# Gated-attention block on eight cores: transposes, evictions and waits of the attention stage reordered, and the loading of W1 moved to another queue

## What is computed

```python
hv = silu(layernorm(x) @ W_h + b_h)                 # 1024 -> 4096
v, gate = hv[..., :HID], hv[..., HID:]
qk = silu(layernorm(x) @ W_qk + b_qk)               # 1024 -> 128, then four heads by gamma, beta
attn = square(relu(einsum('bgid,bgjd->bgij', quad_q, quad_k) / 256 + bias))
quad_out = einsum('bgij,bgje->bgie', attn, v)        # inside a group of 256 tokens
lin_kv   = einsum('bgnd,bgne->bde', lin_k, v) / n    # over the whole sequence
lin_out  = einsum('bgnd,bde->bgne', lin_q, lin_kv)
out = gate * (quad_out + lin_out)
x2 = layernorm(out @ W_o + b_o + 2 x)                # 2048 -> 1024
y  = layernorm(x2 + relu(x2 @ W1 + b1) @ W2 + b2)    # 1024 -> 4096 -> 1024
```

## Time and profile before

| | us |
|---|---|
| median of three runs | 2604.03 |
| lowest and highest of them | 2598.41, 2815.92 |
| the profiled execution, its own time | 2597.35 |
| its span on the slowest core (core 4) | 2595.8 |
| spans of the eight cores | 2580.8 to 2595.8 |

### The profile page before, as it was taken

How to read it: one execution, slowest core, us unless ns; L and a number is a source line. 1 busy time by engine, 2 the same in 40 slices (tenths; PEclk the granted TensorE clock), 3 DMA queues, 4 the chain that set the end, 5 groups by cost and what they waited for, 6 DMA issues and landing times.

```text
span 2595.8 us, 27752 instructions; the slowest of 8 cores (2580.8 to 2595.8 us)
## 1 busy us (share of the span) xinstructions
PE 2083.8 (80%) x9498; PEld 876.5 (34%) x9498; DVE 541.0 (21%) x1127; ACT 731.5 (28%) x1192; POOL 97.0 (4%) x177
## 2 busy tenths in 40 slices
PE   0368888888888827887877876999999989898988
PEld 0123333333333313333333332434343434343433
DVE  0322221222211114334343330011111101010202
ACT  0043343333433203323233232222223131313131
POOL 1001011011111000000000000000000000000000
PEclk9879999999999968787887888999999999999999
DMA  9443344344333374444444425211020202020101
GB/s 142 78 142 111 117 118 118 101 128 117 90 98 102 93 245 157 162 143 162 157 157 165 140 97 154 74 40 57 25 65 17 65 17 74 9 73 25 41 25 49
DMA packets 125172, 256.26 MB, mean 99 GB/s; under 512 B 57614, under 2 KB 66119, under 8 KB 122985
## 3 DMA queue, kind: packets, MB, share of 16 engines
q1 hardware_dynamic: 79642, 121.03, 14.5%
q10 hardware_dynamic: 28800, 100.68, 11.2%
q0 software_dynamic: 16592, 32.78, 8.0%
HBM read 188.64 MB, written 112.20 MB: 116 GB/s over the span
## 4 chain that ended last, share of the span: by engine, by line
PE 72%; ACT 9%; DVE 6%; issue 6%; DMA 3%; another core or an unknown queue 3%; ACTq 1%; DVEq 1%; SPq 0%
PE E L611 18%; PE E L769 17%; PE E L752 16%; PE E L720 11%; PE E L608 3%; ACT h L981 2%; ACT gfm L928 2%; DVE sums L1202 2%; PE E L717 1%; PE E L630 1%; PE E L702 1%; ACT vt L847 1%; DVE pre L1198 1%; DMA xt<-x 1%
## 5 line engine op out<-in xcount | busy, mean ns | idle before, releaser
L752 PE MATMUL E<-xfm,w 128*128 128x512 bf16 x2048 | 461.1, 384 | 75.5 <-ACT h L981 59.4
L611 PE MATMUL E<-wh,nfm 128*128 128x512 bf16 x2048 | 513.0, 396 | 0.0
L769 PE MATMUL E<-w,h 128*128 128x512 bf16 x2048 | 453.2, 379 | 0.0
L752 PEld LDWEIGHTS E<-xfm,w 128*128 128x128 bf16 x2048 | 198.3, 99 | 336.9 <-issue 113.6
L720 PE MATMUL E<-wo,gfm 128*128 128x512 bf16 x1024 | 301.2, 460 | 0.0
L769 PEld LDWEIGHTS E<-w,h 128*128 128x128 bf16 x2048 | 195.2, 98 | 241.2 <-issue 14.6
L611 PEld LDWEIGHTS E<-wh,nfm 128*128 128x128 bf16 x2048 | 184.8, 100 | 258.5 <-issue 88.6
L981 ACT ACTIVATE h<-E,b_fm 128x512 bf16<-128x512 f32 x256 | 173.5, 686 | 321.2 <-PE E L752 321.2
L1235 DVE TENSOR_TENSOR pre<-E,x2r 128x1024 f32<-128x1024 f32 x32 | 39.2, 1225 | 866.5 <-PE E L769 866.5
L720 PEld LDWEIGHTS E<-wo,gfm 128*128 128x128 bf16 x1024 | 111.6, 114 | 179.3 <-issue 112.9
L854 ACT ACTIVATE gt<-E 128x512 f32<-128x512 f32 x128 | 76.5, 597 | 251.1 <-PE E L611 248.3
(11 more groups left out here) (110 smaller groups left out, 1149.6 us busy)
## 6 DMA issues: line engine op xcount, KB each, us to landing
g_sp<-gt ACTq DMA_DIRECT2D x64, 512.0 KB, 2.9
g<-g_sp ACTq DMA_DIRECT2D x64, 512.0 KB, 5.4
xt<-x SPq DMA_DIRECT2D x32, 512.0 KB, 4.3
v_sp<-vt SPq DMA_DIRECT2D x32, 512.0 KB, 2.9
v<-v_sp SPq DMA_DIRECT2D x32, 512.0 KB, 5.0
x2t<-x SPq DMA_DIRECT2D x32, 512.0 KB, 4.2
x_sp<-x2f ACTq DMA_DIRECT2D x32, 512.0 KB, 5.3
x2r<-x_sp SPq DMA_DIRECT2D x32, 512.0 KB, 4.1
```

The lines of the kernel that those rows point to most:

```text
L611: mm = tn.matmul(pslc, T["nfm"][:, sl2 + c * 128:sl2 + (c + 1) * 128], T["wh"][:, c * 2 * HID + s * 512:c * 2 * HID + (s + 1) * 512], star ...
L752: mm = tn.matmul(ps, T["w1"][:, dc * 4096 + ci * 128:dc * 4096 + (ci + 1) * 128], T["xfm3"][:, (Ti % 2) * 4 * DM + dc * 512:(Ti % 2) * 4 * ...
L769: mm = tn.matmul(ps, T["h1"][:, ci * 512 + tt * 128:ci * 512 + (tt + 1) * 128], T["w2"][:, ci * DM + h * 512:ci * DM + (h + 1) * 512], sta ...
```

## The change

- In PE's loop `_emit_x2T(tau - 3)` moves from behind quad and sim to the front of the iteration. It writes the banks E0[1536:2048] and E0[512:1024] and waits, instead of for the whole residual, for its first half only (new counter c_p2h, which the DVE instruction at line 1193 raises).
- `p2_gatedT` alternates between E0[1024:1536] and E0[512:1024], and no longer waits for c_pre2. `p2_Wo` half 0 no longer waits for all four evictions of the gated tile, but for the k-th of them ahead of the matmuls that read it; it waits for the first eviction of the x2T tile, which used its bank.
- On ACT the Sqrt of `p2_ln2(tau)` leaves the end of the iteration and stands one iteration later, behind `_emit_xfmev`.
- The eight W1 loads move from ACT's queue to SP's. SP's first loads are reordered: group 0, q tile 0, v tiles 0 and 1 and x tile 0 first, then groups 1 and 2, q tiles 1 and 2, v tile 2 and x tile 1, then W1, then the loop that loads tiles ahead (v tile 3 and q tile 3 are its first v and q loads).

```diff
-        for g in range(min(3, NG)):
+        load_grp(0)
+        if NT >= 1:
+            load_lq(0)
+            D["v2"].issue(sync, T["v2"][:, 0:HID], v_sp[0:128, :])
+        if NT >= 2:
+            D["v2"].issue(sync, T["v2"][:, HID:2 * HID], v_sp[128:256, :])
+            D["x2"].issue(sync, T["x2t"][:, 0:DM], x_h[0:128, :])
+        for g in range(1, min(3, NG)):
             load_grp(g)
-        for u in range(min(3, NT)):
+        for u in range(1, min(3, NT)):
             load_lq(u)
-        for tau in range(min(3, NT)):
-            D["v2"].issue(sync, T["v2"][:, (tau % 3) * HID:(tau % 3 + 1) * HID],
-                          v_sp[tau * 128:(tau + 1) * 128, :])
-        for tau in range(min(2, NT)):
-            D["x2"].issue(sync, T["x2t"][:, (tau % 2) * DM:(tau % 2 + 1) * DM],
-                          x_h[tau * 128:(tau + 1) * 128, :])
+        if NT >= 3:
+            D["v2"].issue(sync, T["v2"][:, 2 * HID:3 * HID], v_sp[256:384, :])
+        if NT >= 2:
+            D["x2"].issue(sync, T["x2t"][:, DM:2 * DM], x_h[128:256, :])
+        sync.wait_ge(S["sPC1"], 16 * 32)
+        wge(sync, "c_hvmm", 8 * NT)
+        wge(sync, "c_lkvmm", NT)
+        for c in range(DC):
+            if c == 4:
+                sync.wait_ge(S["sW1"], 64)
+            sync.dma_start(
+                out=bass.AP(T["w1"][:].tensor, c * 4096, [[DC * 4096, 128], [1, 4096]]),
+                in_=ap2(w1bf_sp, c * 128 * 4096, [[4096, 128], [1, 4096]]),
+            ).then_inc(S["sW1"], 16)
@@ p2_gatedT
             wge(tn, "c_gated", 4 * u + 4)
-            wge(tn, "c_pre2", u)
+            wge(tn, "c_gtev", 4 * (u - 1) + 4)
             wge(tn, "c_xfmev", 2 * (u - 2) + 2)
@@
-                bank = 1024 + (b % 2) * 512
+                bank = 1024 if b % 2 == 0 else 512
@@ p2_Wo
-            wge(tn, "c_gtev", 4 * u + 4)
+            wge(tn, "c_xfmev", max(2 * (u - 2) + 1, 0))
             wge(tn, "c_pre2", u)
             for h in range(2):
                 if h == 1:
+                    wge(tn, "c_gtev", 4 * u + 4)
@@
                 for k in range(16):
+                    if h == 0 and k % 4 == 0:
+                        wge(tn, "c_gtev", 4 * u + k // 4 + 1)
@@ PE's loop
         for tau in range(NT):
+            _emit_x2T(tn, tau - 3)
             p2_quad(tau)
             if tau % 2 == 0:
                 p2_sim(tau // 2 + 1, tau)
-            _emit_x2T(tn, tau - 3)
@@ _emit_x2T
-        wge(tn, "c_pre2", min(tau + 2, NT))
+        wge(tn, "c_p2h", min(tau + 2, NT))
@@
-            bank = 1024 + b * 512
+            bank = 1536 if b == 0 else 512
@@ ACT: the W1 loads taken out of emit_scalar, p2_ln2 split
-        def p2_ln2(u):
+        def p2_ln2sq(u):
@@
+        def p2_sqrt(u):
+            if not (0 <= u < NT):
+                return
             wge(sc, "c_v2a", u + 1)
             sc.activation(T["s_all"][:, u:u + 1], T["rcp"][:, u:u + 1], AF.Sqrt).then_inc(S["c_s2a"], 1)
@@ ACT's loop
             _emit_xfmev(sc, tau - 3)
+            p2_sqrt(tau - 2)
             if tau % 2 == 0:
                 p2_relu(g + 1)
             p2_gfmev(tau - 1)
@@
-            p2_ln2(tau - 1)
+            p2_ln2sq(tau - 1)
         _emit_xfmev(sc, NT - 3)
+        p2_sqrt(NT - 2)
         p2_gfmev(NT - 1)
-        p2_ln2(NT - 1)
+        p2_ln2sq(NT - 1)
+        p2_sqrt(NT - 1)
@@ DVE, p2_pre2ln
-            vch(ve.scalar_tensor_tensor(T["pre2"][:, (u % 2) * DM:(u % 2) * DM + 512],
+            ve.scalar_tensor_tensor(T["pre2"][:, (u % 2) * DM:(u % 2) * DM + 512],
                                     T["x2t"][:, (u % 2) * DM:(u % 2) * DM + 512],
-                                    2.0, E0[:, 1536:2048], ALU.mult, ALU.add))
+                                    2.0, E0[:, 1536:2048], ALU.mult, ALU.add).then_inc(S["c_p2h"], 1)
             wge(ve, "c_womm", 2 * u + 2)
+            wge(ve, "c_p2h", u + 1)
             vsync()
```

More of the change, by code:

```diff
@@ L250, in build_program @@
         "c_x2bf", "c_x2f", "c_x2T", "c_xfmev",
-        "c_w1mm", "c_h1ev", "c_w2mm", "c_pre3",
+        "c_w1mm", "c_h1ev", "c_w2mm", "c_pre3", "c_p2h",
         "c_v3a", "c_s3a", "c_v3b", "c_ostg", "vq",
@@ L898, in load_gate_half @@
                           g_sp[u * 128:(u + 1) * 128, h * DM:(h + 1) * DM])
[L900 to L909, removed]
         for k in range(min(3, 2 * NT)):
```

## The result

The changed kernel takes 2493 us in the median of its runs against 2601 us for the kernel before in the same series. The ratio is 0.958, with a 95% interval of 0.956 to 0.960: 4.2% faster. The profiled execution took 2491.14 us, 106.2 us less than that of the kernel before. In some executions the cores of one die, or of both, run at a lower clock (in one of the changed kernel four cores at 0.80 to 0.81, 2787 us); such runs are left out of all ratios, and where they would set a median, single times or the time of the profiled run are given instead.

A forecast was written before the change was run, and what follows sets the result against it. PE was taken as the bound, by waiting and by running part of its work at 1.2 GHz. 72.6 + 2.7 + 14 + 11.7 = 101.0 us off 2597.35 gave 2496 us; 8-in-10 range 2465 to 2548.

The forecast's parts named there:

- Odd iterations, the wait: Stage 2, odd iterations and tau = 30: W_o starts at +5.75 us instead of +8.47, 2.72 us saved in each of 16.
- Odd iterations, the clock: W_o half 0, same 16 iterations: full clock kept in 7 of 10, 0.7 x 2.60 = 1.82 us saved each.
- the first rival: Stage 2: the clock falls in every odd iteration too, giving 2525 us; chance 0.25.
- its signs: Iterations 3 to 31 at about 16.4 us, clock near 0.88; first quad near 919; tau = 2 quad waits until about 960.
- Even iterations: Stage 2, 14 even iterations: W_o at +8.37 us instead of +9.37, 1.0 us saved each, 14 us (bounds 0 and 18).
- The clock falls as before: Even iterations: the pause between second and third transpose block grows and the clock still falls; half 0 5 to 7 us.
- Satisfied waits: W_o half 0: four more waits between its matmuls cost nothing when already satisfied.
- The third rival: W_o half 0: its waits break PE's stream, costing 32 us and giving 2528 us; chance 0.08.
- The start of stage 2: First quad near 919 us, but tau = 2 quad waits for v tile 3 until 959.6: 11.7 us saved (bounds 2.7 and 27).
- the traffic beside them: Start of stage 2: 1.5 MB of v, x and gate loads beside the first four W1 loads add some 6 us.
- The other side: Stage 2: gate loads become the bound, slower than before, some 2690 us at about 22 us an iteration; chance 0.03.
- a sign of being wrong: Stage 2: DVE waiting for gate loads would show the prediction wrong; no size given.

The follow-up runs named there:

- e3_sqrt_back: Changed kernel with the Sqrt back at the end of ACT's iteration, ahead of the x2T copies; 2552 us, ratio 0.982 to the kernel before.
- e10_x2T_behind: Changed kernel with the x2T transposes back behind quad and sim; 2516 us, ratio 0.967 to the kernel before.
- e9_pause_odd: Changed kernel with one more wait (for x2bf) ahead of the gated transposes in odd iterations, an empty pause; 2554 us, ratio 0.982 to the kernel before.
- e11_pause_filled: Kernel of e9_pause_odd with 10 extra matmuls, results thrown away, in that pause; 2536 us, ratio 0.975 to the kernel before.
- e4_wo_waits_all: Changed kernel with W_o waiting for all four evictions of the gated tile before it starts; 2533 us, ratio 0.975 to the kernel before.
- e7_w1_spread: Changed kernel with W1 loads in SP's loop, one for each of tau = 2 to 9, behind the next tiles' loads; 2469 us, ratio 0.948 to the kernel before.
- e5_filler: Changed kernel with 15 extra matmuls, results thrown away, in the pause of even iterations 2 to 28; 2475 us, ratio 0.951 to the kernel before.
- e6_relu_late: Changed kernel with ACT's relu of even iterations moved behind the four evictions of the gated tile; 2431.6 us profiled, ratio 0.935 to the kernel before.
- e8_both: Changed kernel with both the relu behind the evictions and W1 loads spread over tau = 2 to 9; 2425 us, ratio 0.931 to the kernel before.
- e12_both_thin: As e8_both, but W1 loads in every third iteration, tau = 2 to 23; 2414.9 and 2414.4 us, ratio 0.929 to the kernel before.

## Why the prediction was right, point by point

Predicted 2496 us, measured 2493 us: the saving was put at 101.0 us and is 106.2 between the two profiled executions. The mechanism was right, two terms of waits and clock in the odd iterations. That the total came so close is partly luck: the loop gave 22 us more than its terms, and the start of stage 2 and a longer stage 1 took 16 of them back.

- **Odd iterations, the wait.** The lead was worked out as 5.75 us and is 5.83; every step shows in the timeline. Copies ended at +3.35 (+3.40 expected), the evictions began at +4.27 (+4.19), the third block at +5.00 (+4.92). e3_sqrt_back and e10_x2T_behind each take a part of the step back, and the lead follows. The saving was put at 2.72 us from one iteration (tau = 13); on the mean of the cores the lead before was 8.77 and not 8.47, so it is 2.94.
- **Odd iterations, the clock.** Taken as kept in 7 of 10; it was kept in all 120 on the eight cores, and at tau = 30 as well. So the first rival fell. The Trainium skill, "TensorE: Matmul & The Clock Gate", Part 4 (PE-mode transpose), says that the full clock doesn't engage for transposes in TensorE's transpose mode. No run here uses that mode; these are plain matmuls, and with 24 of them from one W_o to the next the granted clock in half 0 was 1.00. That the empty pause is the cause is shown by the pair e9_pause_odd and e11_pause_filled, where 119 and 17 of 120 odd iterations lost it. What a fallen clock costs was read as 2.60 us, from one core and from the leads of two iterations; the mean of eight cores is 2.25 in the odd and 2.36 in the even iterations before. A share too low and a price too high partly cancel: 1.82 us forecast, 2.23 measured. So its signs were too weak: it named about 16.4 us an iteration at clock 0.88 (its own sum gives 16.2), and 15.42 us at 0.94 came.
- **Even iterations.** The wait was right: lead 8.37 forecast, 8.44 measured. "The clock falls as before" was right too, but not its price: half 0 went from 6.22 to 5.53 us, 14 x 0.69 = 10 us that the sum did not have. e4_wo_waits_all shows the reason, the missing pause ahead of W_o: with it back, half 0 takes 6.72.
- **Satisfied waits** cost nothing, as said: half 0 takes 3.88 us with four more of them in it. The third rival is out.
- **The start of stage 2** was over-sized: 3.5 us instead of 11.7 on the mean of the cores, inside the bounds. Both landings stand in the trace. The first four W1 loads took from 930.81 to 959.08, 28.3 us, where 22.5 were reckoned; the term that failed is the traffic beside them, taken as 6 us. In 28.3 us at the 269 GB/s of the window from 930 to 960 us some 7.6 MB move, 3.4 MB beside the 4.2 MB of W1 instead of 1.5. v tile 3 was issued at 963.56 and PE went on at 978.77, 15.2 us, against 14.9. The DMA view of its issue (KB, us to landing):

```profile
v<-v_sp SPq DMA_DIRECT2D x1, 512.0 KB, 14.8
```

It landed at 978.3. The chain names a load of q issued at 965.06, but that one is for tile 4 and the quad of tau = 2 doesn't need it; on three other cores the wait is put down to v. Of the 48 us on this core between the first quad and that of tau = 2, 33 pass until SP, which holds the second four W1 loads until the first four have landed, issues v tile 3 at all; the landing is the smaller part. e7_w1_spread shows that the early W1 loads are the cause. The Trainium skill, "DMA: Bandwidth & Descriptors", section Queues, rings and completion order, says that each DMA engine consumes the descriptors of a ring in order. The landings agree: v tile 3 landed behind the last W1 load (975.0), where a 512 KB load landed in 5.4 us in the loop. They don't prove it, since in the kernel before, v loads on the other queue took 14.9 us beside W1 as well.
- **The other side**, gate loads as the bound: DVE waited 8 us for them in all, once, beside W1. The prediction had named such a wait as a sign of being wrong; it came ahead of PE's 28 us wait for v tile 3, which took it up.

By the means of the table: 16 x 5.19 = 83 us from odd iterations and tau = 30, 13 x 1.68 = 22 us from the even ones, and some 6 us from tau = 2 and the tail make the 111.5. The prediction had 89.3 for the same stretch. Of the 22 us more, 6.6 are the clock in the odd iterations (16 x (2.23 - 1.82)), 3.5 their wait (16 x (2.94 - 2.72)), 10 the even half 0, and 2 come from tau = 2 and the tail. Against them stand 8 us less in the start, and a stage 1 that was by chance 8 us longer in the profiled run.

## What to carry to other kernels

In an engine's queue, look at what a cheap instruction waits for, and who stands behind it: a Sqrt of 0.2 us and a relu of 0.6 us, each waiting for another engine, cost 59 and some 57 us here. A pause of TensorE costs its own length and, where the clock falls, nearly as much again (1.83 and 1.71 us in e3_sqrt_back, 2.12 and 1.62 in e9_pause_odd); shortening it, or filling it with matmuls, is worth more than the trace's idle time says. A large load that is needed late belongs behind the small ones of the next tiles in its queue, a piece at a time.

## What the hardware showed that was not expected

- Work that is thrown away can pay: 3.4 us of extra matmuls in 14 iterations made the kernel 18 us faster.
- The same fallen clock cost, on the mean of a kernel's iterations, 1.6 to 2.9 us in the half that followed it (1.1 to 3.2 in single ones). It came back sooner where PE worked without a pause from the third block of transposes on (5.53 against 6.72 us).
- Kernels whose PE hardly paused lost the clock in single odd iterations (12 to 21 of 120 in e5_filler, e6_relu_late, e8_both and e12_both_thin) though the lead was the same as in those that kept it (5.80 to 5.85 against 5.82 to 5.83 us). Why is open; it was not tried.
- The time at which stage 1 ended, with the same code, spread over 25 us across cores and runs. Its cause was not studied either.
